# Turning the expert slots' rows of x with VectorE blocks and SBUF moves instead of TensorE transposes

## The reference

```
x = x + _L0_xattn_ref(_layernorm(x), ctx, ctx, Wq, Wk, Wv, Wfc, bfc)
x = x + _L0_ffn_ref(_layernorm(x), gate_w, Wg, Wu, Wd, cWg, cWu, cWd)

def _routing(x2d, gate_w):                 # 32 experts, the best 4 of each token
    logits = x2d @ gate_w.T
    w, sel = top 4 of sigmoid(logits), with weights softmax(logits) scaled to sum 1
def _moe(x2d, Wg, Wu, Wd, cw):
    g = einsum('th,ehi->eti', x2d, Wg)     # 192 wide per expert, 128 for each pair of experts
    u = einsum('th,ehi->eti', x2d, Wu)
    a = silu(g) * u * cw.T[:, :, None]
    return einsum('eti,eih->th', a, Wd)
out = large + 0.05 * small
```

## Time and profile before

| | |
|---|---|
| time before, median of 3 runs (lowest, highest) | 1076.58 us (1075.65, 1079.62) |
| the profiled execution: its own time | 1080.31 us |
| its span, first to last instruction | 1078.5 us |
| granted TensorE clock, mean over the span | 0.972 |
| PE busy | 1012.3 us, 94% of the span |
| DVE, ACT, POOL busy | 413.5, 368.0, 298.2 us |
| DMA | 146.68 MB, mean 136 GB/s |

### The profile page before, as it was taken

The page is one execution under the profiler, slowest core; times in us unless marked ns, Lnnn a source line. Parts: engine busy times, 40 slices in busy tenths (PEclk is TensorE's granted clock), DMA queues, the critical chain, the costliest instruction groups (busy, mean ns, idle before and its releaser), DMA issues.

```text
span 1078.5 us, 18681 instructions
## 1 busy us (share of the span) xinstructions
PE 1012.3 (94%) x5479; PEld 656.4 (61%) x5480; DVE 413.5 (38%) x1071; ACT 368.0 (34%) x710; POOL 298.2 (28%) x395
## 2 busy tenths in 40 slices
PE   8789999999999977479999999999999999999995
PEld 6557667676665535356666666666666666666662
DVE  4677677777777617811111111111111111111110
ACT  2245464554545526812222222222222222221221
POOL 2111101011020002123434334434333333434342
PEclk9999999999999989589999999999999999999998
DMA  5163234232331019127567676767575677567443
GB/s 202 48 163 75 74 81 104 80 85 83 91 85 50 25 39 365 27 48 228 143 155 202 184 207 167 213 168 206 149 216 157 158 216 224 150 158 216 80 65 55
DMA packets 51755, 146.68 MB, mean 136 GB/s; under 512 B 9856, under 2 KB 19200, under 8 KB 47360
## 3 DMA queue, kind: packets, MB, share of 16 engines
q1 hardware_dynamic: 32016, 103.11, 28.9%
q0 software_dynamic: 17632, 42.74, 20.3%
q10 hardware_dynamic: 2064, 0.26, 0.2%
HBM read 100.73 MB, written 29.36 MB: 121 GB/s over the span
## 4 chain that ended last, share of the span: by engine, by line
PE 56%; issue 0%; DMA 0%; POOL 0%; ACT 0%; DVE 0%; POOLq 0%; ACTq 0%
PE y_ps L1614 19%; PE g_ps L1597 16%; PE u_ps L1597 16%; PE xt_ps L1590 3%; PE at_ps L1606 2%; DMA xg<-xd,gidx 0%; POOL out_x L1501 0%; ACT yb L1533 0%; ACT xT L1522 0%; DVE aT L1555 0%; ACT sg L1526 0%; DVE a L1568 0%; DVE a L1569 0%; POOL gidx L1484 0%; ACTq L1532 0%
## 5 line engine op out<-in xcount | busy, mean ns | idle before, releaser
L1614 PE MATMUL y_ps<-W,aT 128*128 x468 | 215.5, 597 | 0.8 <-DVE aT L1555 0.8
L1501 POOL DMA_INDIRECT out_x<-yb,yidx x78 | 125.3, 1606 | 298.5 <-DMA out_x<-yb,yidx 131.0
L397 ACT ACTIVATE pt<-stp 128x512 f32<-128x512 f32 x256 | 139.1, 596 | 147.3 <-PE stp L723 146.6
L518 DVE TENSOR_REDUCE mx<-s 128x2 f32<-128x512 f32 x256 | 163.4, 682 | 62.1 <-PE s L709 61.5
L1597 PE MATMUL g_ps<-W,xT 128*128 x624 | 182.8, 436 | 1.0 <-ACT xT L1522 1.0
L1597 PE MATMUL u_ps<-W,xT 128*128 x624 | 180.7, 432 | 0.0
L1597 PEld LDWEIGHTS u_ps<-W,xT 128*128 128x128 f32 x624 | 118.6, 190 | 49.5
L1568 DVE TENSOR_TENSOR a<-u_ps,sg 128x192 f32<-128x192 f32 x78 | 27.9, 357 | 290.4 <-ACT sg L1526 290.4
L1526 ACT ACTIVATE sg<-g_ps 128x320 f32<-128x320 f32 x78 | 34.1, 437 | 304.5 <-PE u_ps L1597 304.5
L1597 PEld LDWEIGHTS g_ps<-W,xT 128*128 128x128 f32 x624 | 113.6, 192 | 39.1 <-issue 2.5
L1614 PEld LDWEIGHTS y_ps<-W,aT 128*128 128x128 f32 x468 | 83.2, 191 | 76.1 <-issue 76.1
(11 more groups left out here) (198 smaller groups left out, 930.5 us busy)
## 6 DMA issues: line engine op xcount, KB each, us to landing
W<-in_wts SPq DMA_DIRECT2D x32, 2048.0 KB, 8.3
qst<-q SPq DMA_DIRECT2D x42, 256.0 KB, 5.0
xs<-in_x SPq DMA_DIRECT2D x8, 512.0 KB, 3.8
ctxT<-in_ctx SPq DMA_DIRECT2D x8, 512.0 KB, 4.1
out_x<-xs SPq DMA_DIRECT2D x16, 256.0 KB, 2.3
kst<-k SPq DMA_DIRECT2D x48, 64.0 KB, 2.1
xd<-xs SPq DMA_DIRECT2D x11, 256.0 KB, 2.6
qst<-nm SPq DMA_DIRECT2D x128, 2.0 KB
```

Source lines behind the costliest of these rows:

```text
L397: act.activation(pt[g % 2][:, 2 * (j % 2) + r, :, :], stp[n % STP][:, :, :], ACT.Exp, scale=DH ** -0.5).then_inc(exp_done, 1)
L518: dve.tensor_reduce(mx[j // CH % 2][:, h:2 * G:G], s1[r][:, :, :], AX.X, ALU.max)\
L1501: pool.indirect_dma_start(out[:, :], bass.IndirectOffsetOnAxis(yidx[p][:, :], 0), yb[p][:, :], None, compute_op=ALU.add).then_inc(y_added, ...
L1614: m = pe.matmul(y_ps[:, :], aT[p][:, c, :], W[:, bass.ds(buf, 1), GW + c * D:GW + (c + 1) * D].rearrange("p a d -> p (a d)"), start=(c == ...
```

## The change

`transpose_x` and `x_evac` go, with the PSUM buffers `xt_ps`. In their place, for slot s:

- DVE, `turn(s)`: one transpose instruction on the whole `xg[p]` (128 x 512), which turns each 32x32 block by itself and writes to `xb[p]`, in SBUF. Features are laid so that two blocks are interleaved: 32 tokens x 2 features are one run of 256 bytes.
- ACT, `x_move(s)`: four DMAs, one for each group of 32 tokens (32 partitions of `xb`), spread these runs over the 128 partitions of `xT[p]`. `xT` is now [P, 2, P, 2], so the stationary operand of `gate_up` is read with a step of 2 elements (8 bytes). `gate_up` waits for `x_ready[p]`, the landing of the four DMAs. The rows of the gate and up weights are permuted on the host to match.
- Both run two slots ahead: in slot s, DVE turns slot s+2 between `at_evac(s-1)` and `gated(s)`, and ACT issues the moves of slot s+2 directly behind `silu(s)` and ahead of `y_evac(s-1)`. POOL gathers four slots ahead, and does it behind `add(s-1)` where it was ahead of it.
- The weight `wt` is multiplied in `gated` (an operand of both DVE instructions) instead of in `y_evac`, which becomes a plain copy; `weights_of(s+2)` stands behind `gated(s)`, with a second small instruction for 0.05 * wt.
- SP loads each expert in two pieces, gate and up (1.25 MB) and down (0.75 MB); the second is issued one slot later (`slots_done` at `last + 1`).

```diff
+def load_piece(sp, wts, W, loaded, i, p, n):
+    e, (c0, c1) = i * NW + p, PIECES[n]
+    sp.dma_start(W[:, p, c0:c1], wts[bass.ds(e, 1), :, c0:c1].rearrange("e p n -> (e p) n")).then_inc(loaded[p], DMA)
...
                     sp.wait_ge(slots_done, last)
-                    load_expert(sp, wts, W, w_loaded, i, p)
+                    load_piece(sp, wts, W, w_loaded, i, p, 0)
+                    sp.wait_ge(slots_done, last + 1)
+                    load_piece(sp, wts, W, w_loaded, i, p, 1)
...
             def gather(s, p):
                 if not (isinstance(s, int) and s < 2):
-                    pool.wait_ge(xt_full, s - 1)
+                    pool.wait_ge(turned, s - 1)
                     pool.wait_ge(wt_ready, s - 1)
...
                     for p in range(2):
-                        gather(i * 2 + p + 2, p)
                         add(i * 2 + p - 1, 1 - p)
+                        gather(i * 2 + p + 4, p)
...
-            def x_evac(s, p):
-                act.wait_ge(xt_full, s + 1)
-                act.copy(xT[p][:, :, :], xt_ps[p][:, :].rearrange("p (c t) -> p c t", c=C)).then_inc(xt_empty, 1)
+            def x_move(s, p):
+                act.wait_ge(turned, s + 1)
+                if not (isinstance(s, int) and s < 2):
+                    act.wait_ge(gu_full, s - 1)
+                for i in range(QB):
+                    act.dma_start(xT[p][:, :, i * Q:(i + 1) * Q, :].rearrange("m h r l -> m h (r l)"),
+                                  xb[p][i * Q:(i + 1) * Q, :]).then_inc(x_ready[p], DMA)
...
-                act.wait_ge(wt_ready, s + 1)
...
-                act.activation(yb[p][:, :], y_ps[:, :], ACT.Copy, scale=wt[p][:, :]).then_inc(y_empty, 1)
+                act.copy(yb[p][:, :], y_ps[:, :]).then_inc(y_empty, 1)
...
+            def turn(s, p):
+                dve.wait_ge(x_loaded[p], (s - p) * (DMA // 2) + DMA)
+                if not (isinstance(s, int) and s < 2):
+                    dve.wait_ge(x_ready[p], moved(s - 2, p))
+                dve.transpose(xb[p][:, :].rearrange("p (h r l) -> p h l r", r=Q, l=2), xg[p][:, 0:D]).then_inc(turned, 1)
...
-                dve.tensor_tensor(a[p][:, 0:IL], u_ps[p][:, 0:IL], sg[p][:, 0:IL], ALU.mult)
-                dve.scalar_tensor_tensor(a[p][:, IL:IW], u_ps[p][:, IL:IW], SMALL, sg[p][:, IL:IW], ALU.mult,
+                dve.scalar_tensor_tensor(a[p][:, 0:IL], u_ps[p][:, 0:IL], wt[p][:, 0:1], sg[p][:, 0:IL], ALU.mult,
+                                         ALU.mult)
+                dve.scalar_tensor_tensor(a[p][:, IL:IW], u_ps[p][:, IL:IW], wt[p][:, 1:2], sg[p][:, IL:IW], ALU.mult,
                                          ALU.mult).then_inc(a_ready, 1)
...
             def gate_up(s, p, buf):
-                pe.wait_ge(xt_empty, s + 1)
+                pe.wait_ge(x_ready[p], moved(s, p))
                 for ps_, g in ((g_ps, 0), (u_ps, 1)):
                     for c in range(C):
-                        m = pe.matmul(ps_[p][:, 0:IW], xT[p][:, c, :],
+                        m = pe.matmul(ps_[p][:, 0:IW], xT[p][:, c // 2, :, c % 2],
...
                 gate_up(s, p, buf)
-                transpose_x(s + 1, 1 - p)
                 if not first:
                     down(s - 1, 1 - p, pe.value_load(slot_buf[0:1, bass.ds(s - 1, 1)], min_val=0, max_val=NW - 1))
```

More of the change, by code:

```diff
@@ L1073, in _ @@
         def _(sp):
-            load_expert(sp, wts, W, w_loaded, 0, 0)
+            for n in range(2):
+                load_piece(sp, wts, W, w_loaded, 0, 0, n)
             for t in range(LATE, NT):
@@ L1080, in _ @@
             for p in range(1, NW):
-                load_expert(sp, wts, W, w_loaded, 0, p)
+                for n in range(2):
+                    load_piece(sp, wts, W, w_loaded, 0, p, n)
             for p in range(2):
@@ L1432, in experts @@
         xg = [sb(f"xg{i}", [P, XW], F32) for i in range(2)]
-        wt = [sb(f"wt{i}", [P, 1], F32) for i in range(2)]
-        xT = [sb(f"xT{i}", [P, C, P], F32) for i in range(2)]
+        wt = [sb(f"wt{i}", [P, 2], F32) for i in range(2)]
+        xb = [sb(f"xb{i}", [P, D], F32) for i in range(2)]
+        xT = [sb(f"xT{i}", [P, C // 2, P, 2], F32) for i in range(2)]
         sg = [sb(f"sg{i}", [P, IW], F32) for i in range(2)]
@@ L1438, in experts @@
         yb = [sb(f"yb{i}", [P, D], F32) for i in range(2)]
-        xt_ps = [ps(f"xt_ps{i}", [P, 512]) for i in range(2)]
         g_ps = [ps(f"g_ps{i}", [P, 512]) for i in range(2)]
@@ L1446, in experts @@
         idx_ready, x_loaded = sem("idx_ready"), [sem(f"xg_loaded{i}") for i in range(2)]
-        xt_full, xt_empty, gu_full = sem("xt_full2"), sem("xt_empty2"), sem("gu_full")
+        turned, gu_full = sem("turned"), sem("gu_full")
+        x_ready = [sem(f"x_ready{i}") for i in range(2)]
         wt_ready = sem("wt_ready")
@@ L1453, in experts, with moved @@
         block = ctx.enter_context(nc.Block())
+        def moved(s, p):
+            return (s - p) * (QB * DMA // 2) + QB * DMA
         @block.sync
@@ L1505, in _ @@
                 gather(s, s % 2)
+            gather(4, 0)
             add(0, 0)
+            gather(5, 1)
             n, last = count(pool)
@@ L1549, in _ @@
             y_evac(last + 1, 1)
+            for p in range(2):
+                act.wait_ge(x_ready[p], n * (QB * DMA) + QB * DMA)
+                act.sem_inc(passed, 1)
         @block.vector
@@ L1573, in _ @@
                 dve.memset(a[p][:, IW:IP], 0.0)
+            for p in range(2):
+                turn(p, p)
+                weights_of(p, p)
+            turn(2, 0)
             gated(0, 0)
+            weights_of(2, 0)
             at_evac(0, 0)
+            turn(3, 1)
             gated(1, 1)
+            weights_of(3, 1)
             n, last = count(dve)
@@ L1581, in _ @@
                         at_evac(i * 2 + p - 1, 1 - p)
+                        turn(i * 2 + p + 2, p)
                         gated(i * 2 + p, p)
+                        weights_of(i * 2 + p + 2, p)
             at_evac(last + 1, 1)
```

41 lines of the change are left out of this document (19 added, 22 removed).

## The result

| | before | changed |
|---|---|---|
| median (lowest, highest), 4 runs each | 1076.57 us (1075.65, 1079.62) | 1060.22 us (1058.13, 1064.40) |
| ratio, 95% interval | | 0.9863 (0.9836 to 0.9891) |
| span of the profiled execution | 1078.5 us | 1062.7 us |
| granted TensorE clock over the span | 0.972 | 0.968 |

The forecast was 1047, a gain of 29.7 us; the time lies in the range of 1041 to 1066, but in the part that was kept for the first rival.

What follows compares the result with a forecast made beforehand. PE's own queue was taken as the bound. 1080.31 - 33.1 (transposes of x) + 3.4 (start) = 1050.6 us for the profiled execution; the runs' median, 1076.58 - 29.7, gives 1047. Own range 1042 to 1053; wider range 1041 to 1066.

Steps and rivals of the forecast that it cites:

- the first rival: x late beside the loads of W, a late gather holding `a`; 0.5 us for each of 28 loads, 14 us: 1061; chance 0.12.
- The transposes of x: On PE between up and down: taking them away gains 77 x 0.43 = 33.1 us; the slot becomes 7.22 us.
- rival 5: Transposes of x hidden anyway, as PE meets another wait (`a` or `y_evac`) at once: within 0.5%; chance 0.06.
- When must x be there?: Moves of slot s+2 land at about 9.3 us, gate(s+2) starts at 14.8: 5.5 us are left.
- The start: First slot of the expert stage: gate 2.9 us later, 3.4 taken with PE's low clock, range 2.5 to 4.5.
- the step of 8 bytes: Weight loads of gate and up on PE: stay 190 ns beside matmuls of 269 ns, cost 0; upper bound 380 ns.
- ACT's four issues: Issues of the moves behind silu: 4 x 0.65 = 2.6 us per slot, range 2.4 to 7.2; `y_evac` starts at about 0.7.
- The DMA engines' share: With the moves, engines held 6.5 of 7.22 us per slot, 90%, at 20 ns per 256-byte run; tight, but no bound.
- Rival 4: DMA engines become the bound if 256-byte runs take twice the 28 ns of 512 bytes: 1170; chance 0.03.
- The second's point: Rival 2, weight loads longer than the matmul: costs PE from 269 ns on; at 380 ns 137 us, 1184; chance 0.06.
- The third: Rival 3: pieces of W hold two adds where the whole load held one, 8.4 us each: 67 us, 1114; chance 0.03.
- the pieces: Load of W cut in 5/8 and 3/8, beside the chain of adds in DRAM: counted 0, neither gain nor loss.

Runs made afterwards that it cites:

- the second trace: Kernel before and changed kernel executed and profiled once more, with no edit: before 1077.44 us, changed 1063.53 us, ratio 0.9884.

## Why the prediction missed half the gain

**The transposes of x (33.1 us): right.** 34.0 without loads beside them (77 x 0.433 = 33.3 in the steps, the rest in the step at the loop's end); the step is 7.22 us. Nothing hid behind them (rival 5), since `a` kept 1.23 us of room and `y_evac` was never waited for.

**"When must x be there?": this step failed.** I took the landing of a move, 2.1 us, from a stretch in which no load of W ran, added it to the issue ("land at about 9.3") and found 5.5 us of room. Away from the loads that was right: from the first issue to the last landing it is 4.6 us (median of the changed kernel's 17 slots with no piece of W beside them), so the landing is at 9.6. Beside a load the last of a slot's moves land behind the load. The gate comes 9.8 us behind the first issue, and these are the landings that the traces recorded:

| first issue to last landing, us | slots without a piece of W, median | slots beside a piece, median and longest |
|---|---|---|
| the changed kernel | 4.6 | 8.5, 11.1 |
| loads taken away | 4.6 | 4.8, 6.0 |
| 16 KB, one piece | 6.0 | 11.4, 15.9 |
| 2.5 and 3 KB, a slot apart | 5.0 | 7.1, 8.8 |
| the first piece later | 5.4 | 5.8, 10.7 |
| runs of 512 bytes | 4.9 | 8.7, 10.2 |

Here is one slot that was late. Its moves are issued from 647.81 to 650.48 us (the timeline above), the load at 650.40, and the gate that needs them is due at 657.60. Three windows of the DMA view of the changed kernel (packets, MB, share of 16 engines). From 649.5 to 651.5 us, before the load's packets flow:

```profile
q10 hardware_dynamic: 757, 0.18, 42.1%
q1 hardware_dynamic: 1, 0.01, 2.7%
```

From 652 to 655 us, beside them:

```profile
q1 hardware_dynamic: 90, 0.92, 89.0%
q10 hardware_dynamic: 50, 0.01, 1.8%
```

From 657.4 to 658.6 us, when the load is over:

```profile
q10 hardware_dynamic: 505, 0.12, 47.2%
```

The moves' queue (q10) falls from 757 packets in 2 us to 50 in 3 us, and comes back with 505 in 1.2 us; most of these 505 are already the moves of the next slot, issued from 655.03 us on. Of the 1024 packets of 256 bytes of the slot at hand 863 had started by 652 us, and 51 of its 64 landings (4 moves x 16) were in by 652.51; the last came at 658.47, behind the load, whose packets ran from 651.46 to 657.57. In the middle window the load has 90 packets and the moves 50, and the short ones lie scattered between the long ones: queues take turns row by row here, and a turn of the load's lasts 0.89 x 16 x 3 / 90 = 0.47 us, one of the moves' 18 ns. The Trainium skill (DMA: Bandwidth & Descriptors, Queues, rings and completion order) says that an engine goes round its queues at packet granularity, and puts such a packet at some 9 to 17 descriptors. The windows agree as far as the taking of turns; runs of 9 or more short packets don't show in the middle one, so by the trace a turn was about one row. The windows also show what follows from turns, that a queue with short packets gets a share of the time in proportion to their length. The load's 128 rows are 8 per engine, 8 x 0.47 = 3.8 us of its own; with adds and gathers beside it it fills most of the time between the first window and the third, and what is left of the moves on an engine when it begins gets one short packet per long row. The timeline:

```profile
650.40 7.54 SPq L985 DMA_DIRECT2D W<-in_wts  x2
...
657.27 0.49 PE L1642 MATMUL at_ps<-ident,a 128*128 128x128 f32 x3
...
658.60 0.81 PE L1633 MATMUL g_ps<-W,xT 128*128 x2 [0.84 <-DMA xT<-xb]
```

The gate starts at 658.60 us, 1.0 late, with the second piece of this expert (the x2 of SP's row) only then to come. Eighteen slots lost 0.1 to 1.6 us in this way, 15.1 in all (in this sum a step counts from start to start; the waits of PE's view are some 0.3 us shorter each, for the ends of matmuls are modelled). So in the prediction's own times x was there at 15.6 (658.47 - 642.83) and not at 9.3, and 5.5 us of room were less than none. This is the place and nearly the price of rival 1, which said 14 us for x late beside the loads. But the mechanism I gave it, an add 2.1 us late and the gather behind it, isn't what happened, and that the 14 us (28 loads of 0.5) came so near to 15.1 (18 slots of 0.84) is luck: it is the moves themselves. Late gathers made PE wait for `a` in the kernel with six short DMAs at once (8.7 us in the slots), in the one-piece kernel (3.7, once) and where the weight stands ahead of `gated` (2.4), not in the slots of the changed kernel. Three experiments carry this: no loads, shorter rows of the same bytes, and the same rows issued a little later, each of which takes away 13 to 15 of the 15.1 us. Two ends stay open. How much of the second one is the rows' length and how much their later issue isn't shown. And with runs of 512 bytes, half the packets, the landing beside a piece is no earlier by the median (8.7 us); only the latest ones are.

The error was one of form. "PE waits for a landing, and every landing has the room worked out here" is right, but the landing that I put in was one of another neighbourhood.

**The start (3.4 us forecast, 5.7 and 4.2 measured): under-sized.** The rows of the changed kernel, DVE and ACT's queue, then PE, and PE's before:

```profile
456.31 0.71 DVE L1596 STREAM_TRANSPOSE xb<-xg 128x512 f32<-128x512 f32 x1 [4.48 <-DMA xg<-xd,gidx]
457.06 5.47 ACTq L1542 DMA_DIRECT2D xT<-xb  x8
...
462.69 0.71 DVE L1596 STREAM_TRANSPOSE xb<-xg 128x512 f32<-128x512 f32 x1 [3.12 <-DMA xT<-xb]
```

```profile
462.83 4.63 PE L1633 MATMUL g_ps<-W,xT 128*128 x8 [13.04 <-DMA xT<-xb]
467.26 3.21 PE L1633 MATMUL u_ps<-W,xT 128*128 x8
471.71 0.55 PE L1642 MATMUL at_ps<-ident,a 128*128 128x128 f32 x3 [1.24 <-DVE a L1602]
```

```profile
464.72 4.27 PE L1597 MATMUL g_ps<-W,xT 128*128 x8 [0.97 <-ACT xT L1522]
468.83 2.32 PE L1597 MATMUL u_ps<-W,xT 128*128 x8
```

x(0) is turned at 457.02, its fourth move is issued at about 459.1, and DVE, which waits for the same landing to reuse `xb`, goes on only at 462.69. That is 3.5 us from issue to landing instead of 2.1: the four moves of x(1) and two gathers run beside it, though no run shows that they are the reason. The gate starts 11.24 us behind the stage's start instead of 6.92: 4.3 us, where I had 2.9, and the longer landing is the 1.4 between them. The rest is the clock. The gate then ran at a granted clock of 0.50 and took 4.43 us to up's start, and up's group took 3.21 at 0.72. But before, the first gate too took 4.11 us (464.72 to 468.83, at 0.56), and only up ran at the full clock there (2.32); so the slower matmuls cost 1.3 us in this pair of traces and nothing in the second, where the gate again started 4.6 us later and the sum was 4.2. Splitting the issues gave 2.2 us of the gate's start back.

**The end (0 forecast, 3.5 measured): left out.** The last instructions of DVE, and the last groups of PE:

```profile
1041.13 0.34 DVE L1602 SCALAR_TENSOR_TENSOR a<-u_ps,wt,sg 128x128 f32<-128x128 f32 x1
1042.43 0.15 DVE L1587 COPY wt<-xg 128x1 f32 x1 [0.95 <-DVE a L1602]
1042.62 0.15 DVE L1589 TENSOR_SCALAR wt<-wt 128x1 f32<-128x1 f32 x1
1047.65 0.56 DVE L1579 COPY aT<-at_ps 128x384 f32<-128x384 f32 x1 [4.87 <-issue]
```

```profile
1044.17 0.54 PE L1642 MATMUL at_ps<-ident,a 128*128 128x128 f32 x3 [1.31 <-issue]
1048.36 5.00 PE L1650 MATMUL y_ps<-W,aT 128*128 x6 [3.65 <-DVE aT L1579]
```

The same places before:

```profile
1059.38 0.28 DVE L1569 SCALAR_TENSOR_TENSOR a<-u_ps,sg 128x128 f32<-128x128 f32 x1
...
1064.14 0.56 DVE L1555 COPY aT<-at_ps 128x384 f32<-128x384 f32 x1 [4.48 <-PE at_ps L1606]
1064.85 4.53 PE L1614 MATMUL y_ps<-W,aT 128*128 x6 [0.76 <-DVE aT L1555]
```

From the last `a` of the loop (1041.13) to the copy of `aT` behind it (1047.65) pass 6.5 us; before it was 4.8 (1059.38 to 1064.14). DVE's copy stands 4.9 us behind its last instruction in the loop, and the trace names nothing that it waited for; the two small instructions of `weights_of` that the change put behind `gated` make this start 1.3 us later. PE reached the end of its loop sooner than before, and so waits 3.65 us for `aT` where it was 0.8. Then `down` starts 4.2 us behind the last transposes, not 1.3, and at a lower clock (0.56, before 0.62) takes 0.5 us longer. The kernel with the weight ahead of `gated` got 1.4 to 1.9 us of it back.

**Costed at nothing, and right:** the step of 8 bytes (6 to 7 ns per load, hidden). The Trainium skill (Advanced Engine Details and Errata, Memory Cachelines) wants two hits on each 16-byte line for full performance; 8 bytes give that and 16 don't, and the loads of 197 and 311 ns agree but for the 7 ns above 190. ACT's four issues took 2.67 us (2.6 forecast), and `y_evac` began at 0.52 in the slot above.

**The DMA engines' share: right, and no bound.** Same kernel, 600 to 900 us:

```profile
q0 software_dynamic: 8960, 21.63, 37.6%
q1 hardware_dynamic: 4961, 36.32, 37.0%
q10 hardware_dynamic: 43501, 10.49, 16.3%
```

16.3% of 16 x 300 us over 43501 packets is 18 ns for 256 bytes (forecast 20), and the sum is 90.9% (forecast 90). Rival 4's doubling didn't occur: 512 bytes took 26 ns.

**Rivals 2, 3.** The second's point was wrong: a load of 311 ns didn't cost 42 ns per matmul but 0.12 us once a slot, as loads overlap. A load of 380 ns wasn't seen. The third didn't occur in the changed kernel: its adds beside a piece landed in 5.3 us by the median (5.5 in the second trace), not in 8.4. What resembles it is the kernel with six DMAs at once.

**The sum**, with what was measured, for the stage in the first pair of traces: 620.7 - 34.0 + 15.1 + 5.7 + 3.5 = 611.0. Against the forecast that is 15.1 us for moves beside loads, 2.3 more at the start and 3.5 at the end.

## What to carry to other kernels

A landing time holds for its neighbourhood. Where short packets share the DMA engines with a load of long rows, ask how many turns they need and how long one turn of the load is; the busy share says nothing on that. Cutting the load's rows (here 10 and 6 KB to 2.5 and 3) helps, and so does spreading it, but neither alone was enough: long rows a slot apart cost the slots 15 us, short rows all at once 28, waits for `a` among them. Issuing the long rows a microsecond later took 12.9 of the 15 us away. And the pieces, which I had costed at nothing, decided the sign here: with the expert loaded whole the changed kernel was 4% slower than before. When a loop's body is re-ordered, look at what now stands last in it on each engine, and at the first pass, where nothing is running that could hide a longer chain.
